# Gate logits as extra columns of the value and output products in the second stage

## What is computed

```python
h = _layernorm(x) * (1 + ca) + sa
x = x + ga * _L0_attn_ref(h, L0_attn_w_qkv, L0_attn_w_out)
h = _layernorm(x) * (1 + cb) + sb
x = x + gb * _L0_ffn_ref(h, ...)

def _L0_ffn_ref(x, ...):
    y = _layer_norm(x + _mha(x, Wqkv, bqkv, Wo, bo), g1, be1)
    z = _layer_norm(y + _moe(y, Wg, W1, b1, W2, b2), g2, be2)
    return z

def _moe(x, Wg, W1, b1, W2, b2):      # 8 experts, the best one per token
    logits = xf @ Wg.T
    idx = jnp.argmax(logits, axis=-1)
    for e in range(E):
        m = (idx == e)[:, None].astype(xf.dtype)
        h = jax.nn.relu(xf @ W1[e] + b1[e])
        out = out + m * (h @ W2[e] + b2[e])
```

## Time and profile before

| what | us |
|---|---|
| three runs | 1227.66, 1230.87, 1237.46 |
| median | 1230.87 |
| profiled execution | 1231.36 |
| its span | 1229.5 |

### The profile page before, as it was taken

The page is one execution under the profiler, slowest core; times in us unless marked ns, Lnnn a source line. Parts: engine busy times, 40 slices in busy tenths (PEclk is TensorE's granted clock), DMA queues, the critical chain, the costliest instruction groups (busy, mean ns, idle before and its releaser), DMA issues. The chain is left out here.

```text
span 1229.5 us, 49591 instructions
## 1 busy us (share of the span) xinstructions
PE 1100.4 (90%) x17491; PEld 898.8 (73%) x17491; DVE 955.1 (78%) x4158; ACT 924.4 (75%) x3416; POOL 874.2 (71%) x705
## 2 busy tenths in 40 slices
PE   4699999999999999999999999948998873699991
PEld 2588888888888888888888887626877762688881
DVE  6788898998898898898988987546877754277763
ACT  3689989989989889899899897746866651466660
POOL 3777877877877877778777775554666677178885
PEclk7999999999999999999999999969988975799996
DMA  5776666766766666666767667362242124575100
GB/s 178 207 175 163 177 168 166 183 165 163 182 165 172 174 167 168 176 162 173 177 153 185 162 158 181 79 202 77 78 126 81 67 81 163 155 201 147 57 32 25
DMA packets 110724, 180.50 MB, mean 147 GB/s; under 512 B 19678, under 2 KB 63873, under 8 KB 110352
## 3 DMA queue, kind: packets, MB, share of 16 engines
q1 hardware_dynamic: 102640, 158.14, 49.9%
q0 software_dynamic: 6400, 16.82, 3.8%
q10 hardware_dynamic: 1440, 2.36, 0.8%
HBM read 34.81 MB, written 24.73 MB: 48 GB/s over the span
## 5 line engine op out<-in xcount | busy, mean ns | idle before, releaser
L593 POOL TENSOR_TENSOR qk<-mm,sw 128x1024 f32<-128x1024 f32 x128 | 304.3, 2378 | 102.8 <-DMA sw<-mm 102.5
L673 ACT ACTIVATE pr<-sm,mn 128x96 f32<-128x96 f32 x1024 | 368.6, 371 | 0.3 <-DVE mn L490 0.3
L599 POOL TENSOR_TENSOR pr<-pr,ri 128x768 f32<-128x768 f32 x128 | 189.5, 1480 | 67.9 <-DVE ri L517 67.2
L478 DVE TENSOR_TENSOR mm<-bank,cos 128x512 f32<-128x512 f32 x256 | 175.3, 685 | 72.9 <-PE bank L321 60.2
L673 ACT ACTIVATION_READ_ACCUMULATOR pr<-sm,mn 128x1 f32 x1024 | 202.1, 197 | 0.0
L490 DVE CUSTOM_DVE_ANT_0 sm<-bank,msk 128x96 f32<-128x96 f32 x1024 | 190.9, 251 | 3.7 <-PE bank L347 3.7
L479 DVE TENSOR_TENSOR mm<-bank,sin 128x512 f32<-128x512 f32 x256 | 174.0, 680 | 0.0
L374 PE MATMUL bank<-pT,vw 96*64 96x64 f32 x4096 | 148.3, 226 | 0.0
L374 PEld LDWEIGHTS bank<-pT,vw 96*64 96x64 f32 x4096 | 130.6, 138 | 17.2 <-issue 6.0
L664 ACT ACTIVATE pT<-bank 96x512 f32<-96x512 f32 x256 | 137.3, 588 | 0.0
L389 PE MATMUL bank<-ident,pr 128*96 128x128 f32 x1024 | 132.7, 272 | 0.0
(11 more groups left out here) (201 smaller groups left out, 2489.6 us busy)
## 6 DMA issues: line engine op xcount, KB each, us to landing
sw<-mm SPq DMA_DIRECT2D x512, 128.0 KB, 2.4
vw<-vn SPq DMA_DIRECT2D x128, 192.0 KB, 2.6
vw<-vn SPq DMA_DIRECT2D x128, 128.0 KB, 2.4
rr<-sorted_scratch SPq DMA_DIRECT2D x72, 192.5 KB, 2.7
vw<-vn SPq DMA_DIRECT2D x96, 64.0 KB, 2.3
xt<-in_x SPq DMA_DIRECT2D x16, 256.0 KB, 4.1
x_scratch<-x SPq DMA_DIRECT2D x16, 256.0 KB, 2.6
rr<-x_scratch SPq DMA_DIRECT2D x16, 256.0 KB, 3.2
```

Of the source, the lines that this page charges most:

```text
L478: dve.tensor_tensor(mm[s % 2][:, 0, j, :], PJ[u % 2][:, :], cos[:, :], ALU.mult)
L593: pool.tensor_tensor(qk[i % 2][:, :, 32:], mm[i % 2][:, 0, :, :], sw[i % 2][:, :, :], ALU.add)\
L599: pool.tensor_tensor(t, t, ri[i % 2][:, :].unsqueeze(2).to_broadcast([P, 8, WK]), ALU.mult)\
L673: ins = act.activation(pr[i % 2][:, h, p, :], ms_[i % 2][:, h, p, :], ACT.Exp, scale=-1.0, bias=mn[i % 2][:, h, p:p + 1], accum_out=sums[i ...
```

## The change

The gate's weights are folded into two products that exist anyway. The logits of a token are (y * g1 + be1) @ Wg.T with y = (r - mean(r)) * rstd and r = h2 + attention output. With gate weights scaled by g1 and centred over the channels, the part (r - mean) @ ... is a sum of eight extra columns of the v product (for h2) and eight extra columns of the output product (woT times those weights). So:

- v and wo become 136 columns wide (wve, woe), their results take two neighbouring banks each (the last four banks are two tensors of 1024 columns, two groups of 136 columns in each bank). The ring is now a table of positions: a wide use starts at an even position and waits for the last users of both banks.
- ScalarE copies the eight columns of v into the widened h2 (L1236 in the new numbering). The residual add is then 4 x 136 columns, and its last eight are the logits but for the factor rstd and a constant row (lgb).
- VectorE makes the logits from uu with a multiply and an add (one copy before), in the slot of the residual add, s-4, after POOL's norm; rank, slot numbers and scatter move from s-6 to s-5, the loop ends one slot sooner (LAST = NQ + 5).
- The transposes t3, the yT copy and the logit products lg are gone. The four one-column products of W1 move to the bank of wo(s-3), in the same slot, and the bias add to the head of VectorE's slot.
- hT is a plain copy (its bias is in fbn, the permutation in the oT copy). prepare() stands ahead of the loop, and a new gate() with small operations in its place; TensorE and ScalarE make the extra weights before the loop.
- POOL's norm waits for one more semaphore (the logits' multiply of s-6).

```diff
@@ banks @@
-        banks = [top.enter_context(nc.psum_tensor(f"bank{i}", [P, 512], F32)) for i in range(8)]
+        banks = [top.enter_context(nc.psum_tensor(f"bank{i}", [P, 512], F32)) for i in range(4)]
+        wide = [top.enter_context(nc.psum_tensor(f"bank{4 + 2 * i}", [P, 1024], F32)) for i in range(2)]
+        banks += [wide[i // 2][:, 512 * (i % 2):512 * (i % 2) + 512] for i in range(4)]
@@ phase2: the ring @@
-    FIRST, LAST = -3, NQ + 6
-
-    order = []
+    FIRST, LAST = -3, NQ + 5
+
+    r_use, r_pos, last_use, r_prev, pos = {}, {}, {}, {}, 0
     for s in range(FIRST, LAST):
-        order += [w for w in (("t1", s), ("q", s), ("k", s), ("rk", s - 6), ("pt", s - 2), ("v", s), ("t3", s - 5),
-                              ("lg", s - 5), ("wo", s - 3)) if 0 <= w[1] < NQ]
-    r_use = {w: n for n, w in enumerate(order)}
+        for kind, u in (("t1", s), ("q", s), ("k", s), ("rk", s - 5), ("pt", s - 2), ("v", s), ("wo", s - 3)):
+            if 0 <= u < NQ:
+                size = 2 if kind in ("v", "wo") else 1
+                pos += pos % size
+                held = [(pos + n) % 4 for n in range(size)]
+                r_use[kind, u], r_pos[kind, u] = len(r_use), pos % 4
+                r_prev[kind, u] = {last_use[n] for n in held if n in last_use}
+                last_use.update({n: (kind, u) for n in held})
+                pos += size
+    emptied = {"t1": s_he, "q": s_qe, "k": s_ke, "pt": s_pe, "v": s_ve, "wo": s_u, "rk": s_rkd}
@@ tensor: bank @@
-                n = r_use[w]
-                if n >= 4:
-                    kind, v = order[n - 4]
+                for kind, v in sorted(r_prev[w]):
                     pe.wait_ge(emptied[kind], v + 1)
-                return RING[n % 4]
+                return ring(*w)
@@ tensor: v and wo @@
-                    dst = bank("v", u)
+                    bank("v", u)
+                    dst = blocks("v", u)
                     for g in range(4):
-                        ins = pe.matmul(dst[:, g * C:(g + 1) * C], hT[u % 2][:, g * P:(g + 1) * P], wf[:, 2 * C:],
+                        ins = pe.matmul(dst[:, g // 2, g % 2, :], hT[u % 2][:, g * P:(g + 1) * P], wve[:, :],
                                         start=True, stop=True)
...
+                    e = u - 2
+                    if 0 <= e < NE:
+                        pe.wait_ge(s_ws[e % 2], 16 * (e // 2 + 1))
+                        for c in range(4):
+                            pe.matmul(pair("wo", u)[:, 0, 2 * CE + c:2 * CE + c + 1], w1s[e % 2][:, c * P:(c + 1) * P],
+                                      gcol[:, 1:2], start=True, stop=True)
                     for j in range(4):
-                        ins = pe.matmul(dst[:, j * C:(j + 1) * C], oT[u % 2][:, j * P:(j + 1) * P], wfo,
+                        ins = pe.matmul(dst[:, j // 2, j % 2, :], oT[u % 2][:, j * P:(j + 1) * P], woe[:, :],
                                         start=True, stop=True)
@@ scalar @@
-                    act.wait_ge(s_bx, e - 1)
+                    act.wait_ge(s_r, r_use["wo", e] + 1)
...
-                    act.activation(va[u % 3][:, :, :], ring("v", u)[:, :].rearrange("p (g c) -> p g c", g=4), ACT.Copy)\
-                        .then_inc(s_ve, 1)
-                u = s - 5
-                if quad(u):
-                    act.wait_ge(s_r, r_use[("t3", u)] + 1)
-                    if u >= 1:
-                        act.wait_ge(s_r, r_use[("lg", u - 1)] + 1)
-                    act.activation(yT[:, :], ring("t3", u)[:, :], ACT.Identity, scale=gcol[:, 0:1], bias=gcol[:, 1:2])\
-                        .then_inc(s_ye, 1)
+                    act.activation(halves(va[u % 3][:, :, :]), blocks("v", u)[:, :, :, 0:C], ACT.Copy)
+                    act.activation(halves(h2[u % 7][:, :, C:]), blocks("v", u)[:, :, :, C:], ACT.Copy).then_inc(s_ve, 1)
@@ vector: gate, uu, logits @@
+            def gate():
+                dve.wait_ge(s_eo, 2)
+                dve.tensor_scalar(wgs[:, :], wg, gcol[:, 0:1], None, ALU.mult).then_inc(s_do, 1)
+                dve.tensor_copy(lgb[:, :], X[2][:, NE:2 * NE]).then_inc(s_do, 1)
+                dve.tensor_tensor(fbn[:, :], fb, X[2][:, 2 * NE:2 * NE + 3], ALU.add).then_inc(s_do, 1)
+                dve.wait_ge(s_do, 12)
+                dve.scalar_tensor_tensor(out=wve[:, C:], in0=X[2][:, 0:NE], scalar=-1.0 / C, in1=wgs[:, :],
+                                         op0=ALU.mult, op1=ALU.add).then_inc(s_do, 1)
+                dve.wait_ge(s_eo, 3)
+                dve.tensor_copy(woe[:, C:], X[3][:, 0:NE]).then_inc(s_do, 1)
...
-                    dve.tensor_tensor(uu[u % 2][:, :, :], ring("wo", u)[:, :].rearrange("p (j c) -> p j c", j=4),
-                                      h2[u % 7][:, :, :], ALU.add).then_inc(s_u, 1)
+                    e = u - 2
+                    if 0 <= e < NE:
+                        dve.tensor_tensor(b1t[:, 4 * e:4 * e + 4], b1t[:, 4 * e:4 * e + 4],
+                                          pair("wo", u)[:, 0, 2 * CE:2 * CE + 4], ALU.add).then_inc(s_bx, 1)
+                    dve.tensor_tensor(halves(uu[u % 2][:, :, :]), blocks("wo", u), halves(h2[u % 7][:, :, :]), ALU.add)\
+                        .then_inc(s_u, 1)
...
-                u = s - 6
+                u = s - 5
...
-                    dve.tensor_copy(lg[:, :, :], ring("lg", u)[:, 0:4 * NE].rearrange("p (j e) -> p j e", j=4))\
+                    dve.tensor_tensor(lg[:, :, :], uu[u % 2][:, :, C:], rs[s % 2][:, 1, :].unsqueeze(2).to_broadcast([P, 4, NE]),
+                                      ALU.mult).then_inc(s_le, 1)
+                    dve.wait_ge(s_le, 2 * u + 1)
+                    dve.tensor_tensor(lg[:, :, :], lg[:, :, :], lgb[:, :].unsqueeze(1).to_broadcast([P, 4, NE]), ALU.add)\
                         .then_inc(s_le, 1)
             dve.wait_ge(s_po, 3)
+            prepare()
             for s in range(FIRST, LAST):
                 if s == FIRST + 1:
-                    prepare()
+                    gate()
@@ gpsimd @@
                     if quad(s - 6):
                         pool.wait_ge(s_cy, s - 5)
+                        pool.wait_ge(s_le, 2 * (s - 6) + 1)
...
-                u = s - 6
+                u = s - 5
```

102 lines of the change are left out of this document (51 added, 51 removed).

## The result

The changed kernel takes 1248.4 us (median of 4 runs, 1245.3 to 1252.1) beside 1230.7 for the kernel before (1227.7 to 1237.5): ratio 1.0127, 95% interval [1.010, 1.0155]. The forecast was 1226 with a range of 1214 to 1242. The profiled execution took 1247.32 us with a span of 1245.4, 15.9 more than before.

A forecast was written before the change was run, and what follows sets the result against it. TensorE (busy 10.11 of 10.60 us a slot) and VectorE (9.83) were taken as full. Loop -6.9, clock +9.2, drain -5.2 and -1.8, slots 0 to 4 +0.3 sum to -4.4: 1226 us, range 1214 to 1242.

The forecast's parts named there:

- The loop: Slots 5 to 12: v waits for VectorE's rank-bank read, closing a loop over v, ScalarE and w1l of 11.96 us.
- TensorE isn't in the loop at full clock: Slots 5 to 12: wo products end before w1l starts, 3.3 us behind v's end against 3.9.
- Sum at full clock: 116.1 against 123.0, -6.9: Slots 5 to 14: eight loop slots (95.7 us) plus slots 13 and 14 (20.4), against the kernel before.
- clock term: Slots 5 to 14: TensorE's clock falls at the v wait, 1.15 us a slot in eight of ten, +9.2 us.
- The last two slots: Slots 13 and 14: no w1l, VectorE sets about 10.2 us each, 20.4 us together.
- Fetch gaps: TensorE gaps ended by issue, left out of the sum since the v wait can cover them; up to 3 us if not.
- Slots 0 to 4: Extra ScalarE copy adds 0.15 us a slot, the unpermuted hT copy gives back about 0.1: +0.3 us.
- Drain: After the last slots: eight scatters instead of twelve behind the last norm, -5.2 us, and POOL's wait mostly back, -1.8.
- Rival 1: Slots 5 to 14: the loop binds but TensorE's clock holds; 1217 us, chance 0.17.
- Rival 3: Slots 5 to 14: the clock stays low from the v wait, slots of 15 us; 1251 us, chance 0.13.
- Rival 2: Slots 5 to 14: the ring wait is hidden, about 8 us less in the ten slots; 1215 us, chance 0.08.

The follow-up runs named there:

- e7: Changed kernel with ScalarE converting w1h ahead of the oT copies; ratio to the kernel before 1.0225 in a late session, 1.0166 in a first one.
- e3_again: Changed kernel with 16 idle bf16 products on TensorE ahead of v, from the sixth slot on; ratio to the kernel before 1.0055.
- after_third: The changed kernel itself run once more, nothing altered; ratio to the kernel before 1.0133.
- e10: e8_both with 64 idle products (128 instructions) on TensorE ahead of the loop; 1223.5 us, ratio to the kernel before 0.9938.
- e8_both: Changed kernel with VectorE's rank-bank reads ahead of h2 and ScalarE's w1h conversion ahead of the oT copies; ratio to the kernel before 1.0003.
- e1: Changed kernel with the rank products behind v in TensorE's order and the ring; ratio to the kernel before 0.9957 (late session), 1.0025 (first).
- e6: Changed kernel with VectorE's two reads of the rank bank moved ahead of h2's two operations; ratio to the kernel before 1.0011 (late session).

## Why the prediction was wrong

- **The loop: right in place and in size.** v waits 2.25 us in each slot; undisturbed the loop takes 12.0 us (forecast 11.96). It held v, foT, w1h, w1l as walked. The forecast's "TensorE isn't in the loop at full clock" is right but narrow: e7 shows the path over wo as long at 0.82.
- **The failed step: "Sum at full clock: 116.1 against 123.0, -6.9".** It sets ten undisturbed slots of after against ten slots of before as they were, with low clock, late instructions and longer operations in them, and puts these at nothing for after, but for the clock. The undisturbed slot of before takes 10.60 us, ten of them 106.0: 17.0 us of the 123.0 are disturbances. Like against like, the loop is worth 116.1 - 106.0 = +10.1, not -6.9. Measured were 139.7 us, where the forecast had 125.3 with its clock term. e3_again shows the missing terms, since there almost nothing is left to the clock: its eight turns are 11.4 us above the sum, 7.5 of late instructions, 2.7 of h2 beside GpSimd's add and 1.2 of b2r, which the walk around the loop left out since the sample slot has none. A loop passes such things on. They are not simply those of before, though: the first profile after has 1.5 us of late instructions where before had 8.6, but four long h2 operations where before had one of that length and two shorter ones. The last two slots, forecast at 20.4, took 24.8.
- **The clock term: +9.2.** What e3_again gives back by raising the clock from 0.80 or 0.81 to 0.96 is 8.2 (from the first profile) or 9.3 (from after_third); the turns leave 12.4 and 5.0 for it. So the sum was about right, partly by luck: a turn at 0.66 to 0.70 costs 2.2 to 2.6, twice the 1.15 of the forecast, while other turns keep the full clock. The page of the Trainium skill that the prediction weighed (TensorE: Matmul & The Clock Gate, "A second HAM failure mode: psum-queue depth-cycling") speaks of a clock that swings at such idles, as it does here; the measured part fits the forecast's number and that for all ten slots alike. The fillers move the instruction stream too (e3_again has 7.3 us more late time than the first profile), so the split is good to a few us only.
- **Fetch gaps: left out, "up to 3".** Right for the first profile in size (1.5 us in ten slots), too low for after_third (7.0) and e3_again (8.8). Whether a wait covers some isn't shown; those that show lengthen the turn, and in late sessions the half microseconds come behind the wait.
- **Slots 0 to 4: +0.3, measured +2.7** and +5.8 in after_third. Two boundaries of the instruction stream fell into pv and scores, which e10 shows by moving them: 39.2.
- **Drain: -7.0, measured -6.5** and -6.0. Eight scatters behind the last norm:

```profile
1047.06 0.20 POOL L971 TENSOR_TENSOR fnb<-fnb,frs 128x8 f32<-128x8 f32 x1
1047.95 1.09 POOL L994 DMA_INDIRECT sorted_scratch<-rr,slot  x1 [0.69 <-issue]
...
1057.23 0.97 POOL L994 DMA_INDIRECT sorted_scratch<-rr,slot  x1 [0.31 <-issue]
```

- **Rivals.** Rival 1, the clock holds, gave 1217: the clock fell to 0.80, and e3_again, at 0.96, still takes 1237.8. Rival 3 gave 1251 us and decides from a mean slot of 14.2; the mean was 13.97 and the time 1248. Its number was near, its mechanism not: the clock recovers within slots (1.00 from 882 to 897), and the length is the loop's with the disturbances in it. Rival 2, the wait hidden, would have won about 8 us in the slots; e8_both, where it is gone, wins nothing there. VectorE is busy for 103.1 of the 124.0 us and waits for TensorE's rank products and scores for 12.7; what holds the slot was not tested.

What stays open: what the wait alone costs the kernel before in a first session; how the 17 us of disturbances in the kernel before divide (8.6 us are late instructions, but they overlap with the low clock); and what makes TensorE's instructions come half a microsecond late in some sessions.

## What to carry to other kernels

When a change closes a loop over several engines, add its undisturbed length to nothing but undisturbed lengths, and then put on top of it the disturbances that the stretch can meet (low clock, late instructions, two engines' operations side by side, work that comes once): a loop has little slack to swallow them. A bank that is released late by another engine costs a wait in each turn; put its user behind that reader's turn in the order (e1) or its last reader earlier (e6): each took back what the wait had cost in slots 5 to 14. Look for the places of late instructions before explaining small differences between two kernels: 128 idle instructions ahead of the loop (e10) were worth more here than the change.

## What was not expected of the hardware

- In first sessions TensorE's instructions come late only at places 256 of its records (some 126 matmuls and as many weight loads) apart: 1 to 3 us when the place lies in a group of 64 short products; moving these places by 128 instructions took slots 0 to 4 from 46.4 to 39.2 us.
- In some sessions the same program has another kind of late instructions beside these, half a microsecond each at any place: 20.0 us in slots 5 to 14 against 8.6, and 1285 us against 1231 in all.
- A gap of 2.10 us in TensorE's work in e8_both is followed by a slot at a clock of 0.65, with a second gap of 2.01 in it; that slot takes 13.43 us, and 8.29 in e10, without the gaps and at a clock of 1.00.
- VectorE's second 128x512 operation on h2 takes up to 1.73 us when it runs beside GpSimd's 128x512 add, and 0.69 without it.
